# Row moves on POOL dealt out anew over the slots of an attention and expert kernel, with some loads of SP in another order

## The reference, cut to what matters

```python
xn = layernorm(x)                                  # 32 x 256 x 128
Q, K, V = xn @ Wq + bq, xn @ Wk, xn @ Wv           # 16 heads of 64
R = xn @ Wr + br                                   # 16 heads x 10 basis weights
extra[t, p] = sum_n R[t, n] * b_nd[n, t - p]       # position bias, 0 <= t - p < 128
W = softmax(Q K^T / 8 + bias + extra); A = (W V) @ Wproj + bproj
# experts: the best 2 of 8 for each of 8192 rows
top = top_k(xn @ router_w.T, 2); w = softmax(top.values)
y_e = gelu(xn @ w1[e].T + b1[e]) @ w2[e].T + b2[e]
out = x + A + sum_k w_k * y_top_k
```

## Time and profile before

| | us |
|---|---|
| median of 3 runs | 1433.98 |
| lowest and highest | 1433.4, 1434.38 |
| the profiled execution | 1427.99 |
| its span in the trace | 1426.3 |
| PE busy in it | 1315.0 |
| ACT, DVE, POOL busy | 948.8, 892.6, 866.3 |

### The profile page before, as it was taken

The page is one execution under the profiler, slowest core; times in us unless marked ns, Lnnn a source line. Parts: engine busy times, 40 slices in busy tenths (PEclk is TensorE's granted clock), DMA queues, the critical chain, the costliest instruction groups (busy, mean ns, idle before and its releaser), DMA issues. The chain is left out here.

```text
span 1426.3 us, 34890 instructions
## 1 busy us (share of the span) xinstructions
PE 1315.0 (92%) x10589; PEld 1108.5 (78%) x10589; DVE 892.6 (63%) x3652; ACT 948.8 (67%) x2967; POOL 866.3 (61%) x1637
## 2 busy tenths in 40 slices
PE   5789998899999999998899999999999999999997
PEld 2478886787777777776799999987787787777775
DVE  5478886677677767776111221127787777777775
ACT  2477776677777767776444445447777777777774
POOL 6456665777777777775223322327777777777673
PEclk9899999999999999999899999999999999999999
DMA  7687777667766766776556555637777777777772
GB/s 236 196 241 206 227 220 217 199 199 220 201 191 199 206 201 191 205 205 195 156 167 168 162 163 165 170 97 199 200 209 201 195 205 205 207 204 212 198 213 63
DMA packets 456609, 274.95 MB, mean 193 GB/s; under 512 B 21180, under 2 KB 436839, under 8 KB 456424
## 3 DMA queue, kind: packets, MB, share of 16 engines
q1 hardware_dynamic: 448232, 255.92, 63.4%
q0 software_dynamic: 8192, 16.79, 3.9%
HBM read 124.19 MB, written 133.19 MB: 180 GB/s over the span
## 5 line engine op out<-in xcount | busy, mean ns | idle before, releaser
L926 ACT ACTIVATE prob<-logit,low 128x128 f32<-128x128 f32 x1024 | 401.7, 395 | 39.8 <-DVE low L1265 28.4
L1265 DVE CUSTOM_DVE_ANT_0 logit<-ps,extra 128x128 f32<-128x128 f32 x1024 | 255.3, 286 | 73.3 <-PE ps L1541 46.5
L788 POOL TENSOR_SCALAR prob<-prob,inv 128x128 f32<-128x128 f32 x512 | 189.3, 370 | 170.2 <-DVE inv L1282 168.6
L1247 DVE TENSOR_TENSOR probT<-ps,keep 128x512 f32<-128x512 f32 x256 | 175.8, 687 | 80.0 <-PE ps L1528 77.6
L916 ACT COPY qk<-ps 128x512 f32<-128x512 f32 x256 | 150.3, 587 | 100.6 <-PE ps L1439 72.5
L1541 PEld LDWEIGHTS ps<-qk 64*128 64x128 f32 x2048 | 167.0, 188 | 59.1 <-issue 47.2
L1528 PE MATMUL ps<-ident,prob 128*128 128x128 f32 x1024 | 156.8, 275 | 53.6 <-POOL prob L790 53.0
L1541 PE MATMUL ps<-qk 64*128 64x256 f32 (+1 forms) x2048 | 203.4, 338 | 0.0
L1560 PE MATMUL ps<-probT,val 128*64 128x256 f32 (+1 forms) x2048 | 196.0, 334 | 3.5 <-DVE acc L1325 3.5
L926 ACT ACTIVATION_READ_ACCUMULATOR prob<-logit,low 128x1 f32 x1024 | 194.4, 190 | 0.0
L790 POOL TENSOR_SCALAR prob<-prob,inv 128x128 f32<-128x128 f32 x512 | 188.1, 367 | 0.0
(11 more groups left out here) (185 smaller groups left out, 2610.5 us busy)
## 6 DMA issues: line engine op xcount, KB each, us to landing
skew<-gst SPq DMA_DIRECT2D x384, 256.0 KB
extra<-skew SPq DMA_DIRECT2D x256, 256.0 KB, 3.3
w2b<-w_d SPq DMA_DIRECT2D x39, 320.0 KB, 3.4
rT<-r_hi SPq DMA_DIRECT2D x128, 80.0 KB
w1raw<-w_d SPq DMA_DIRECT2D x39, 258.0 KB, 2.8
placed<-x_place SPq DMA_DIRECT2D x39, 256.0 KB, 3.2
y_place<-yrow SPq DMA_DIRECT2D x39, 256.0 KB, 2.2
rT<-r_lo SPq DMA_DIRECT2D x64, 80.0 KB
```

The source lines that it names most:

```text
L788: nc.gpsimd.tensor_scalar(prob[:, h, 0:P], prob[:, h, 0:P], inv[:, h, 0:1], 1.0, ALU.mult, ALU.mult).then_inc(norm_made, 1)
L926: ins = nc.scalar.activation(prob[:, h % PB, cols], logit[:, h % LB, cols], ACT.Exp, scale=-1.0, bias=low[:, h % LB, t:t + 1], accum_out=t ...
L1247: nc.vector.tensor_tensor(probT[:, h:h + 2, 0:2 * P], src, keep[:, 0:2 * P].unsqueeze(1).broadcast_to([P, 2, 2 * P]), ALU.mult)
L1265: ins = nc.vector.tensor_tensor_reduce(out=logit[:, h % LB, cols], in0=ps[:, b + n, cols], in1=extra[:, h, cols], scale=1.0, scalar=BIG, o ...
```

## The change

- The tables: a slot 0 now has 1 move and a slot 1, 2 or 3 has 3 (`MOVES`, 10 in a sequence). Spreads run from slot 17 to 67 and fetches from 73 to 123, where they ran from 19 to 68 and from 73 to 125.
- In slot 0 the one move stands ahead of the norms. Then come norms, the bias addition of the first 16 slots, other moves, and `round_weights` last.
- SP writes pads in slots 14 to 16 (3, 3 and 2) and no longer in 14 to 17 (2 each).
- At the start SP loads w2 and fills the skew area ahead of the twelve basis writes, and not behind them.
- `first_rows` is called in slot 69 ahead of unit (3,1). Within it the rows come ahead of the weights of block 1 and the second weights of block 0.
- `xb_hi` and `xb_lo` of even blocks get memory of their own behind `w1raw`; those of odd blocks stay over gst. The waits for `skew_out` stay.

```diff
-        xb_hi = sb("xb_hi", [P, 2, BANK], F32R)
-        xb_lo = sb("xb_lo", [P, 2, BANK], F32R)
+        xb_hi1 = sb("xb_hi1", [P, BANK], F32R)
+        xb_lo1 = sb("xb_lo1", [P, BANK], F32R)
+        top[0] = logit_at
...
         w1raw = sb("w1raw", [P, 2, RAW1])
+        xb_hi0 = sb("xb_hi0", [P, BANK], F32R)
+        xb_lo0 = sb("xb_lo0", [P, BANK], F32R)
+        xb_hi, xb_lo = (xb_hi0, xb_hi1), (xb_lo0, xb_lo1)
...
-        SPREAD_FROM, SPREAD_DS = 19, 4 * (HALF - 1) + 1 - 19
-        FETCH_FROM, FETCH_DS = 4 * HALF + 1, DS - 2 - (4 * HALF + 1)
-        spread_at = [SPREAD_FROM + m * SPREAD_DS // (TILES * TOP) for m in range(TILES * TOP)]
-        fetch_at = [FETCH_FROM + m * FETCH_DS // (TILES * TOP) for m in range(TILES * TOP)]
+        MOVES = (1, 3, 3, 3)
+
+        def moves_from(q):
+            at_q = [q + n for n in range(DS - q) for _ in range(MOVES[(q + n) % QUADS])]
+            return at_q[:TILES * TOP]
+
+        spread_at, fetch_at = moves_from(4 * 4 + 1), moves_from(4 * HALF + 1)
...
-                if 14 <= q < 14 + NX // 2:
-                    zero_pads(2 * (q - 14))
+                if 14 <= q < 17:
+                    zero_pads(range(3 * (q - 14), min(3 * (q - 13), NX)))
...
                 others(4 * i + 1)
+                if i == HALF - 1:
+                    first_rows()
                 positions(i, POSITIONS_OWN[2:])
                 others(4 * i + 2)
                 if more:
                     positions(i + 1, POSITIONS_AHEAD[:2])
-                    if i == HALF - 1:
-                        first_rows()
...
                     if heads:
-                        if d > 0:
-                            moves(4 * i + d, 0)
+                        moves(4 * i + d, 0)
...
-                    if heads and 4 * i + d < BLOCKS:
-                        add_bias(4 * i + d)
+                    if heads:
+                        if 4 * i + d < BLOCKS:
+                            add_bias(4 * i + d)
+                        moves(4 * i + d, 1)
                     if d == 0 and heads and more:
                         round_weights(i + 1)
-                    if heads:
-                        if d == 0:
-                            moves(4 * i, 0)
-                        moves(4 * i + d, 1)
```

More of the change, by code:

```diff
@@ L395, in build @@
         DS = 4 * B
-        SPREAD_FROM, SPREAD_DS = 19, 4 * (HALF - 1) + 1 - 19
-        FETCH_FROM, FETCH_DS = 4 * HALF + 1, DS - 2 - (4 * HALF + 1)
-        spread_at = [SPREAD_FROM + m * SPREAD_DS // (TILES * TOP) for m in range(TILES * TOP)]
-        fetch_at = [FETCH_FROM + m * FETCH_DS // (TILES * TOP) for m in range(TILES * TOP)]
+        MOVES = (1, 3, 3, 3)
[3 more added lines that the diff above has]
+        spread_at, fetch_at = moves_from(4 * 4 + 1), moves_from(4 * HALF + 1)
+        assert spread_at[-1] < 4 * HALF - 3 and fetch_at[-1] < DS - 3
         rows_at = [spread_at[4 * j] for j in range(TILES // 2)]
@@ L447, in _ @@
             sp.dma_start(wv_r[:, :], Wv).then_inc(wv_in, 16)
+            sp.dma_start(w2_raw[:, :, :], w2.rearrange("e h f -> h e f")).then_inc(w2_in, 16)
+            sp.wait_ge(fill_made, 1)
+            sp.dma_start(skew_rows(0, 0, H, P, P, ROW),
+                         fill[:, :].unsqueeze(1).broadcast_to([P, H, P])).then_inc(filled, 16)
             sp.wait_ge(brev_split, 2)
@@ L456, in _ @@
                                  src[:, :].bitcast(F32)).then_inc(basis_in, 16)
-            sp.wait_ge(fill_made, 1)
-            sp.dma_start(skew_rows(0, 0, H, P, P, ROW),
-                         fill[:, :].unsqueeze(1).broadcast_to([P, H, P])).then_inc(filled, 16)
-            sp.dma_start(w2_raw[:, :, :], w2.rearrange("e h f -> h e f")).then_inc(w2_in, 16)
             def write_unit(i, g, t):
@@ L514, in zero_block, with zero_pads @@
                 sp.dma_start(zero_v[n, :, :, :], zeros).then_inc(zeroed, 16)
-            def zero_pads(first_expert):
+            def zero_pads(experts_of):
                 sp.wait_ge(owner_made, 1)
-                for e in (first_expert, first_expert + 1):
+                for e in experts_of:
                     row = sp.value_load(pad_row[0:1, e:e + 1], min_val=0, max_val=PLACES * BANK)
@@ L640, in first_rows @@
                 first_weights(0, 0)
-                first_weights(1, 1)
-                second_weights(0, 0)
                 for n in range(XR):
@@ L646, in first_rows @@
                     block_rows(b, b)
+                first_weights(1, 1)
+                second_weights(0, 0)
             for i in range(HALF):
@@ L983, in high_part @@
                 wait_from(act, hid_psum, (b - 1) * FC)
-                nc.scalar.copy(xb_hi[:, u, :], ps[:, XB_BANK[u], :]).then_inc(xb_high, 1)
+                nc.scalar.copy(xb_hi[u][:, :], ps[:, XB_BANK[u], :]).then_inc(xb_high, 1)
             deviations(0, 0, 16)
@@ L1349, in low_x @@
                 wait_from(dve, hid_psum, (b - 1) * FC)
-                nc.vector.tensor_tensor(xb_lo[:, u, :], ps[:, XB_BANK[u], :], xb_hi[:, u, :].bitcast(F32),
+                nc.vector.tensor_tensor(xb_lo[u][:, :], ps[:, XB_BANK[u], :], xb_hi[u][:, :].bitcast(F32),
                                         ALU.subtract).then_inc(xb_low, 1)
@@ L1457, in expert_in @@
                     product(ps[:, H_BANK[c], :], ((w1b[:, u, f], w1b[:, u, FF + c * P:FF + (c + 1) * P]),
-                                                  (xb_hi[:, u, :], xb_lo[:, u, :]))).then_inc(hid_psum, 1)
+                                                  (xb_hi[u][:, :], xb_lo[u][:, :]))).then_inc(hid_psum, 1)
             def expert_out(b, u, k):
```

## The result

The changed kernel takes **1382.84 us** (median of 4 runs, 1380.37 to 1389.08) against 1434.18 (4 runs, 1433.4 to 1436.44) for the kernel before: ratio 0.9646, 95% interval 0.9611 to 0.9681. The forecast was 1380, 1369 to 1397. The profiled execution took 1381.54 us, span 1379.1, so 47.2 us less span than before.

The account below looks back on a forecast made before the run. PE, busy 92% of the span, was taken as the bound, losing 53.0 us waiting for POOL's norms. Terms -51.8 + 1 - 3 + 1.5 - 2 = -54.3 took 1433.98 to about 1380 us, range 1369 to 1397.

Parts of the forecast that it names:

- part 1: POOL's row moves: two or three fewer behind the rounding remove PE's waits for norms in slot 1, -51.8 us.
- with 1 us to spare: Slot 1: moves removed save 2.5 or 3.8 us against waits of 1.5 and 2.8, so both go whole.
- 0.64 is free: Slot 0: a third move ahead makes POOL's norms 0.64 us late, which costs PE nothing (tolerance 1.15).
- rival 2: Slot 0 takes over the stall: split, three moves, norms; 17 us if PE's tolerance is smaller, 1396 us, chance 0.06.
- The reads: DVE's logits of quad 2 need SP's position reads, whose slack falls to about zero: +1 us, ends 0 and 13.
- part 4: Into the experts: first weights and rows are asked for earlier, in SP's pause; -2 us, ends -6 and +5.
- Part 2: Start: w2 load and skew fill go ahead of basis writes, so rT lands sooner; -3 us, ends -5 and +1.
- its issue (the last two from 33.00) doesn't move: Start: SP still issues rT at the same time though 3 MB now stand ahead of the basis writes.
- Part 3: First moves from slot 17: norms of quad 16 stall some 7 us for pads, mostly absorbed; +1.5, ends -2 and +6.
- 1: Rival: the position reads become the bound, 13 us or up to 1 us each; 1392 to 1405 us, chance 0.13.
- 4: Rival: slower, as three moves in slot 1 delay the read of quad 2's bias; 1457 us, chance 0.03.
- 3: Rival: the two one-time places go wrong together (+6, +5, start +1); 1395 us, chance 0.08.
- 5: Rival: norms of slot 1 stay late because r_raw, not the moves, holds POOL back; 1420 us, chance 0.02.

Follow-up runs that it names:

- x_2332: Changed kernel with two moves in slot 0 and two in slot 3 instead of one and three: 1380.80 us, beside 1385.79 for the changed kernel.
- x_order: Kernel before with only the new order of POOL's instructions (old tables, start, pads, expert loads): 1384.07 us, again 1385.67.
- x_start_b: Changed kernel with the old start order (basis writes, then fill, then w2), second run of x_start: 1384.17 us; first run 1394.03.
- x_best: Changed kernel with (2, 3, 3, 2) moves for fetches, old table and padding slots for rows: 1386.80 us, beside 1397.44 for the changed kernel.
- x_behind17: Changed kernel with slot 17's three moves all behind its norms: 1396.19 us, ratio 0.9702 to the kernel before.
- x_first: Changed kernel with first_rows() back behind the positions of slot 2, weights ahead of rows: 1386.93 us, beside 1385.79 for the changed kernel.

## Why the prediction was right, and where it wasn't

- **What bounds the kernel, and part 1 (-51.8):** right. With two or three moves fewer behind the rounding, PE's wait for norms went from 53.0 to 3.8 us outside the one stall (11.6 - 7.8), and the two stretches with moves gave 47.4 us, 49.7 with the experts and the end. The rest of a sequence without the wait was 31.11 in the forecast; the shorter sequences now take 30.95. But "with 1 us to spare" was luck in every second sequence of the first attention part: the one move left behind the rounding waits 1.13 us for DVE's rows, which the forecast didn't count, the norms are 1.28 us late, and the tolerance is 1.3.
- **"0.64 is free" (slot 0):** half right. The tolerance of 1.15 read in the earlier trace rows holds there, and reaches to 1.28. But while the rows are spread the lateness was 1.78 in every second sequence and about 0.9 in the others, not 0.64; behind the experts it was mostly 0.1. The forecast read the 0.63 of idle time in the earlier trace rows at one sequence and took it for all. In the longer sequence of the changed kernel the first move of slot 3 waits 2.56 us for DVE's rows, and what follows on POOL runs on without a pause into the norms of slot 0; that this makes the difference of the two is read from the trace, not tested. Each such wait costs 0.4 us; x_2332, which doesn't have it, shows it. That is rival 2 in small: some 3 us, not 17.
- **The reads (+1):** DVE waits for reads 20.1 us in 13 pieces, after 11.4 in 5; one of 5.34 belongs to part 4. PE has little of the other twelve: the sequences with the two longest (1.85 and 1.88 us) take 31.28 and 32.02 us where their like take 30.95 and 31.83. The step held. The forecast named a rule of the Trainium skill (DMA: Bandwidth & Descriptors, Queues, rings and completion order), that a DMA engine serves its queue rows in turn. It had priced it at 0.5 us in every sequence, 13 in all. The traces agree that DVE waits for reads more often, not that PE pays.
- **Part 2 (-3, ends -5 and +1):** wrong, +3.9 in the first trace. The step that failed is "its issue (the last two from 33.00) doesn't move". The forecast weighed only the landing of rT and not whether SP can go on issuing: the first of the twelve basis issues was held for 9.77 us, and rT went out 8.5 us later (37.68 against 29.16). What this costs is 2.2 us at the basis product: it comes at 44.2 to 44.7 us in all nine traces with the new start and at 42.0 to 42.5 in all five with the old. The rest of the 3.9 is the second gate, which the forecast didn't have: the write of the turned w2 landed 10.1 us after its issue in this trace and 8.4 in the one before. Over the 14 traces it takes 8.4 to 10.1 whatever the start (10.0 in x_order, 8.7 in the changed kernel's second trace), and the first logits follow within 0.2 us of it each time. So that part isn't the order's. What the new start costs in the end isn't settled: x_start_b, without it, is no faster, and x_order is 6.1 us ahead of x_best at quad 20.
- **Part 3 (+1.5 with the waits after it, so -1.3 in the table):** 0.0. The stall was to be some 7 us and is 7.75; that it mostly vanishes in the waits behind it is what x_behind17 shows. The size was off: from quad 0 to quad 18 the changed kernel is 3.0 us behind (152.2 and 149.1), not 1.5. POOL's first move, which waits for the pads, started at 219.95, where the forecast had the last pads at 216.5; the late start of 3.9 us accounts for it.
- **Part 4 (-2):** -1.4, and 2.6 by x_first. The last slot was to get 5.4 us longer, and DVE's wait there is 5.34; ACT's shrinks from 9.83 to 3.88. The experts' own memory was set at 0. The experts take 280.9 us with it and 281.7 before, but 280.7 and 281.0 in the two runs of x_order, which lacks it, so no gain of it shows.
- **The median:** the forecast's 1380 lies 2.8 below it. On spans the miss is 7.1 us, nearly all of it the start. The changed kernel's profiled run stands only 1.3 us below its median (1381.54, 1382.84), where the forecast kept 6; that took back 4.7 of the miss and was luck. In the third group the same kernel took 1397.44, just outside the range.
- **Rivals:** 1 and 4 didn't come, 2 in small, 3 not (only the start went wrong), 5 not.

## What to carry to other kernels

A long instruction between a producer's input and a waiting engine counts by its place, not by the number of them: take it out of the one slot where the chain is tight, and either a new order or a new table does it. Here the order alone took off as much as the whole change. Measure the tolerance first, and in each stage (here 1.3 us in the first attention part, 0.8 in most sequences of the second), and count for the fullest slot what earlier slots defer into it. Before bulk loads are put ahead of small transfers on one queue, ask whether the engine that issues can go on, and what it issues next. And compare variants beside an unaltered kernel on the same chip: the same kernel differed by 15 us between groups, more than any variant differed from it within one.

## What the runs showed of the hardware

**An issue can hold its engine.** A small basis write takes SP 0.7 to 0.9 us to issue. Issued right behind the load of w2 (2 MB) and the fill (1 MB), the first one took 9.55 to 9.88 us in all nine traces with the new start, and it ended within 0.02 us of the landing of w2 each time; the next took 0.8 again. But the same two transfers don't always hold what follows. In the kernel before, the first issue of rT stands right behind them and took 1.36 us. There the DMA engines had been idle before the two (share 0.03); here the loads of two attention weights (`wqk_r`, `wv_r`) were still under way. Which of these makes the difference no run shows.

**The same write, 8.4 to 10.1 us.** The write of the turned w2, the same bytes at the same place of the program, landed 8.4 to 8.7 us after its issue in eleven traces and 9.6 to 10.1 in three.

**The same kernel in three places.** The changed kernel took 1382.84, 1385.79 and 1397.44 us in its first measurement and in the second and third groups, the kernel before 1434.18, 1433.82 and 1439.79. Between quads 28 and 44 the third group took 128.5 us where the second took 125.6. In slot 2 of each sequence ACT's copy of the values comes 2.1 and 1.0 us late in turn, where the second group has 0.2 and 0.1. DVE's and ACT's timelines in the second group, at one place of the program:

```profile
355.10 0.29 DVE L1272 CUSTOM_DVE_ANT_0 logit<-ps,extra 128x128 f32<-128x128 f32 x1 [0.33 <-PE ps L1549]
...
354.03 0.58 ACT L886 COPY val<-ps 128x512 f32<-128x512 f32 x1 [0.22 <-PE ps L1447]
```

And at the same place in the third group:

```profile
356.22 0.29 DVE L1272 CUSTOM_DVE_ANT_0 logit<-ps,extra 128x128 f32<-128x128 f32 x1 [1.36 <-PE ps L1549]
...
355.92 0.59 ACT L886 COPY val<-ps 128x512 f32<-128x512 f32 x1 [2.12 <-remote]
```

PE's own rows stand at the same times in both (its transposes at 349.86 and 357.2), and the wait appears only from the sequence in which the moves begin. DVE's next inverse and POOL's norms come 1.2 us later for it. The first group has the same late copies (2.0 to 2.2 us in x_start), and x_start_b in the second has none of them (0.2), so they go with the chip or the occasion and not with the kernel; the runs don't part these two. Both runs of x_order (1384.07 and 1385.67) stood in groups with late copies. Why the two engines wait isn't known: no run takes that wait alone away, and it stays open.
